# Attention block on one core: the first projection between two query tiles, the residual amid the copies, and the next batch's x tiles and statistics earlier

## The chip, the cores and the metric

The kernel runs on one core of a Trainium2 chip. Times are device microseconds (us) of that core. TensorE (PE) multiplies matrices into PSUM, VectorE (DVE), ScalarE (ACT) and GpSimd (POOL) work on tiles, and SyncE (SP) issues transfers. An engine runs its instructions in the order in which they are written; between engines only semaphores set an order.

## The reference, cut to what matters

```python
def _group_norm(x, scale, bias):                  # 32 groups of 16 channels, over all 1024 tokens
    mean, var = xg.mean(axis=(1, 3)), xg.var(axis=(1, 3))
    return ((xg - mean) * rsqrt(var + EPS)).reshape(B, T, C) * scale + bias

h = _group_norm(x)                                # x: 16 batches of 1024 tokens, 512 channels, fp32
q, k, v = split(h @ qkv_w + qkv_b, 3, axis=-1)    # weight 512 x 1536
q, k, v = (t.reshape(B * 8, 1024, 64) for t in (q * s, k * s, v))
a = softmax(q @ k.T) @ v
out = x + (a.reshape(B, T, C) @ proj_w + proj_b)
```

Because the reshape comes without a transpose, each of the 8 heads of a batch is one block of 128 tokens, whose 512 channels are cut into 8 chunks of 64: 1024 positions of width 64 that attend to one another.

## The kernel before, in words

A batch has 8 blocks (heads), taken as 4 pairs. A block's score matrix has 1024 rows, made 128 at a time: this is a *slot*. A batch has 64 slots, `k` = 0 to 63, the program 1024. All engines run the same loop by *steps* of two slots (even `k`); each has its own list of what it does at which `k`, written out by hand. A pair takes 16 slots, so eight steps; I call them by `k` mod 16: step 0, 2, ..., 14. The stretch "step 4" begins when PE starts the scores of a slot with `k` mod 16 = 4.

In each step PE multiplies the scores of the two slots (L353), which go into two PSUM tiles `s_ps`. Then, in step 2, 6, 10 and 14, it multiplies probabilities by values (`attend`, L382). In step 0, 4, 8 and 12 it transposes two small tiles (L364) and then runs the *large units* of the table `LARGE`: the values `v` of the present pair, the query and key tiles `qk` 0 to 7 of the **next** pair, and the projection of the two blocks of the **previous** pair (`proj` 0 and 1). Twelve units per pair share two PSUM banks, `c_ps0` and `c_ps1`, strictly by turns (`bank`). A unit may start when the unit two places before it has been emptied (`await_bank`).

Who empties a bank depends on the unit. A `qk` tile is emptied by ACT (`stage_qk`): a key tile in one instruction of 128 partitions (L490), a query tile in four of 64 partitions (L495); only the last of them tells PE. `QK_TILES` makes units 0, 1, 4 and 5 query tiles and the rest key tiles. A `proj` unit is emptied by DVE (`take_proj`, L662), which adds it to the residual `x_res`. That tile is loaded by SP (`load_residual`, L306), after the store of the block before has landed, and then given the bias by POOL (`add_bias`, L812); DVE waits for both.

For each slot DVE takes the largest score (L639), ACT the exponential (L475) and DVE turns the result into `turned` in blocks of 32 (L622). After four slots (a *half*) SP moves 16 pieces of `turned` to `probs_t` (L318, `move_half`), which finishes the transpose for `attend`. For the next batch SP loads eight x tiles into one buffer `x_next` (L299), DVE turns each (L611), takes statistics (L707) and aggregates them (L712); PE averages over the groups in `k` = 44 and 46 (L445), reading `s_ps0`, so that the scores after it wait until DVE has taken the product (L717, L724).

Of the kernel before, what the change touches and what calls it, by code (L numbers as in the profile page):

```python
# [11 lines left out]
P = 128  # L12
BATCHES, TOKENS, C = 16, 1024, 512
BLOCKS = TOKENS // P
# [12 lines left out]
Q = 32  # L27
# [4 lines left out]

TURN_STEPS = [4, 8, 12, 20, 24, 28, 36, 40]
STAT_STEPS = [8, 12, 20, 24, 28, 36, 40, 42]
AGGREGATE_SLOT = 42
GROUP_MEAN_SLOT = 44
GROUP_VAR_SLOT = 46

LARGE = {0: [("v", 0), ("v", 1)], 4: [("proj", 0), ("qk", 0), ("qk", 1)],
         8: [("qk", 2), ("qk", 3), ("qk", 4), ("qk", 5)], 12: [("qk", 6), ("proj", 1), ("qk", 7)]}
QK_TILES = [0, 1, 4, 5, 2, 3, 6, 7]
START_TILES = [4, 5, 6, 7, 0, 1, 2, 3]
# [34 lines left out]
def attention_block(nc, x, norm_scale, norm_bias, qkv_w, qkv_b, proj_w, proj_b, out):  # L79
# [3 lines left out]
    with ExitStack() as ctx:  # L83
# [194 lines left out]
        @block.sync  # L278
        def _(sp):
            def load_weight_rows(sp, part, t):  # L280
                cols = slice(part * C, (part + 1) * C)
                for z in range(QUADS):
                    rows = qkv_w[P * z + Q * t:P * z + Q * (t + 1), cols]
                    sp.dma_start(w_stage[t][Q * z:Q * (z + 1), cols], rows).then_inc(w_loaded[part], 16)

            for n in range(2):
                load_x_start(sp, n)
            for part in (1, 0, 2):
                for t in range(KT):
                    load_weight_rows(sp, part, t)  # L290
            for t in range(KT):
                sp.dma_start(pw_stage[t], proj_w[t * P:(t + 1) * P, :]).then_inc(pw_loaded, 16)

            def load_x_tile(b, u):
                if within(b, BATCHES - 1):
                    at_least(sp, xt_turned, BLOCKS * (b + 1) + u)
                    for z in range(QUADS):
                        part = x_t[b + 1, u, :, P * z:P * (z + 1)].rearrange("(a i) c -> i a c", i=Q)
                        sp.dma_start(x_next[Q * z:Q * (z + 1), :].rearrange("p (a c) -> p a c", a=QUADS), part  # L299
                                     ).then_inc(xs_loaded, 16)  # L300

            def load_residual(b, n):
                h = BLOCKS * b + n
                if within(h, N_BLOCKS):
                    at_least(sp, stored, 16 * h)
                    sp.dma_start(x_res[:, :], x_t[b + n // BLOCKS, n % BLOCKS]).then_inc(x_loaded, 16)  # L306

            def move_half(b, k):
                n = (k - MOVE_LAG) // HALF
                half = 2 * BLOCKS * b + n  # L310
                if not within(half, N_HALVES):
                    return
                at_least(sp, probs_turned, HALF * half + HALF)
                at_least(sp, pv_done, half - 1)
                for step in range(QUADS):
                    for a in range(QUADS):
                        to = (a + step) % QUADS
                        sp.dma_start(probs_t[n % 2][Q * to:Q * (to + 1), a, :],  # L318
                                     turned[n % 2][Q * a:Q * (a + 1), to, :]).then_inc(moved[n % 2][to], 16)

            def slot(b, k):
                if k % HALF == MOVE_LAG % HALF:
                    move_half(b, k)
                if k % 16 == 1:
                    load_residual(b, 2 * (k // 16) - 2)
                if k % 16 == 9:
                    load_residual(b, 2 * (k // 16) - 1)
                if k == 1:
                    load_x_tile(b, 0)
                if k - 2 in TURN_STEPS[:-1]:  # L330
                    load_x_tile(b, TURN_STEPS.index(k - 2) + 1)

            batches(slot)
            sp.wait_ge(stored, 16 * N_BLOCKS)

# [135 lines left out]
        def _(act):  # L471
# [61 lines left out]
            def step(b, k):  # L533
                s = SPB * b + k
                if k % HALF == EVAC_LAG % HALF and within(s - EVAC_LAG, N_SLOTS):
                    take_inverse(b, k)
                if within(s, N_SLOTS):
                    softmax_exp(b, k)
                if k % 16 == 8:
                    stage_qk(b, k, 0)  # L540
                if within(s, N_SLOTS):
                    softmax_exp(b, k + 1)
                if k % 16 == 12:
                    stage_qk(b, k, 0)
                if k % 16 == 4:
                    stage_qk(b, k, 1)
                if k % 16 == 4 or k % 16 == 12:
                    stage_qk(b, k, 2)
                if k % 16 == 8:
                    stage_qk(b, k, 1)  # L550
                    stage_qk(b, k, 2)
                    stage_qk(b, k, 3)
                if k % 16 == 6:
                    store(b, 2 * (k // 16) - 2)
                if k % 16 == 14:
                    store(b, 2 * (k // 16) - 1)
                if k % 16 == 0 and within(made_pair(b, k), N_PAIRS):
                    norm_x(b, k, 0)
                    norm_x(b, k, 1)
                if before_start(b) and k == GROUP_VAR_SLOT:  # L560
                    round_qkv_weights(1)
                    round_qkv_weights(0)
                if before_start(b) and k == GROUP_VAR_SLOT + 4:
                    round_qkv_weights(2)
                if b == 0 and k == 0:
                    round_proj_weights()
# [14 lines left out]
        def _(dve):  # L581
# [16 lines left out]
                nc.vector.tensor_scalar(qk_bias[:, KT:2 * KT], qk_bias[:, KT:2 * KT], CH ** -0.5, None,  # L598
                                        ALU.mult).then_inc(bias_scaled, 1)

            def turn_x(b, u):
                if before_start(b):
                    dve.wait_ge(x_start_loaded[u // 2], 16 * QUADS)
                    tile = x_start[u // 2][:, u % 2 * C:(u % 2 + 1) * C]
                else:
                    dve.wait_ge(xs_loaded, 16 * QUADS * (BLOCKS * b + u + 1))
                    tile = x_next[:, :]
                if u % 2 == 0:
                    at_least(dve, h_split, 2 * (PPB * b + u // 2 + 1))
                dst = xt_sb[:, u // 2, :, u % 2 * P:(u % 2 + 1) * P].rearrange("p k (a i) -> p k a i", i=Q)  # L610
                nc.vector.transpose(dst, tile.rearrange("p (a k j) -> p k a j", a=QUADS, k=KT)).then_inc(xt_turned, 1)  # L611

# [51 lines left out]
            def step(b, k):  # L664
# [7 lines left out]
                    turn(b, k)  # L672
                if k % 16 == 0:
                    take_v(b, k, 0)
                if k % 16 == 4:
                    take_proj(b, k, 0)
                if b == 0 and k == 2:
                    split_proj_weights()
                if within(s, N_SLOTS):
                    turn(b, k + 1)  # L680
                if k % 16 == 0:
                    take_v(b, k, 1)
                if k % 16 == 12:
                    take_proj(b, k, 1)
                if k % HALF == HALF - 2 and within(s, N_SLOTS):
                    invert(b, k)
# [5 lines left out]
                if before_start(b) and k == GROUP_VAR_SLOT + 4:  # L692
                    split_qkv_weights(2)

            def statistics(b, k):
                if not within(b + 1, BATCHES):
                    return
                nb = b + 1
                if k in TURN_STEPS:
                    turn_x(b, TURN_STEPS.index(k))  # L700
                if k in STAT_STEPS:
                    u = STAT_STEPS.index(k)
                    dve.wait_ge(xt_turned, BLOCKS * nb + u + 1)
                    if u == 0:
                        at_least(dve, aggregated, 2 * nb)
                    for t in range(KT):
                        last = nc.vector.bn_stats(bn[:, t, u, :], xt_sb[:, u // 2, t, u % 2 * P:(u % 2 + 1) * P])  # L707
                    last.then_inc(bn_done, 1)
                if k == AGGREGATE_SLOT:
                    at_least(dve, bn_done, BLOCKS * (nb + 1))  # L710
                    for t in range(KT):
# [18 lines left out]
        def _(pool):  # L730
# [95 lines left out]
            def four_slots(b, k):  # L826
                m, pair = k % 16, k // 16
                if m == 4:
                    add_bias(b, 2 * pair - 2)
                if m == 12:  # L830
                    add_bias(b, 2 * pair - 1)
                if m == 12:
                    split_qk(b, k, LARGE[m][0][1])
                if m == 8:
                    split_qk(b, k, LARGE[m][0][1])
                    split_qk(b, k, LARGE[m][1][1])
                split_attn(b, (k - EVAC_LAG) // HALF)
                if m == 0 and within(made_pair(b, k), N_PAIRS):
                    split_h(b, k)
                if m == 4:  # L840
                    split_qk(b, k, LARGE[m][1][1])
                if m == 4 or m == 12:
                    split_qk(b, k, LARGE[m][2][1])
                if m == 8:
                    split_qk(b, k, LARGE[m][2][1])
                    split_qk(b, k, LARGE[m][3][1])
                widen_inverse(b, k)
                if k == GROUP_MEAN_SLOT and within(b + 1, BATCHES):
                    affine(b)
# [23 lines left out]
```

## Time and profile before

| | us |
|---|---|
| median of 3 runs (3390.82 to 3396.11) | 3392.52 |
| the profiled execution | 3391.84 |
| its span | 3390.1 |
| busy: PE, DVE, ACT, POOL | 3299.4, 2892.6, 2011.0, 1654.7 |

The span is what lies between the first and the last instruction of the program in the profile; the profiled execution took 1.7 us more. Busy shares are means over the whole span. All 16 batches do the same work, so a stretch of one pair, read instruction by instruction, stands for the others.

### The profile page before, as it was taken

The page shows a single profiled execution, that of the slowest core. Times are in us where ns is not written, and L with a number is a line of the kernel's source. Part 1 is how long each engine was busy: PE and PEld are TensorE (multiplying, and loading weights), DVE is VectorE, ACT ScalarE, POOL GpSimd, SP SyncE. Part 2 cuts the span into 40 slices and gives each one's busy share as a digit, 9 for nine tenths or more (in the row PEclk, how much of TensorE's full clock was granted, in tenths as well). Part 3 has the DMA queues.
Part 4 walks back from the last instruction along what each step waited for, and adds up shares of the span by engine and source line. Part 5 has one row for each costly group of instructions (what it writes and reads, how often), then busy time and mean ns, then how long its engine had stood idle before and what let it go on. Part 6 is the DMA issues. An engine that isn't in the chain of part 4 may idle for free.

```text
span 3390.1 us, 66951 instructions
## 1 busy us (share of the span) xinstructions
PE 3299.4 (97%) x24128; PEld 2488.8 (73%) x24128; DVE 2892.6 (85%) x3601; ACT 2011.0 (59%) x3857; POOL 1654.7 (49%) x2762
## 2 busy tenths in 40 slices
PE   5999999999999999999999999999999999999998
PEld 4777777777777777777777777777777777777775
DVE  5888889888888888888888888888888888888886
ACT  4565565665665656656656666556566565665663
POOL 3454454544545545545545455445454554454552
PEclk9999999999999999999999999999999999999999
DMA  5888878788887888878788787878878888788777
GB/s 115 195 188 197 193 188 203 184 198 192 190 202 184 199 192 193 201 184 201 188 194 202 185 198 188 194 195 190 198 188 197 195 190 201 184 197 194 185 186 183
DMA packets 312633, 646.84 MB, mean 191 GB/s; under 512 B 80624, under 2 KB 146160, under 8 KB 312304
## 3 DMA queue, kind: packets, MB, share of 16 engines
q1 hardware_dynamic: 289216, 607.43, 76.4%
q10 hardware_dynamic: 23088, 35.14, 3.1%
q8 instruction: 192, 3.15, 0.4%
q14 instruction: 137, 1.12, 0.1%
HBM read 71.84 MB, written 33.55 MB: 31 GB/s over the span
## 4 chain that ended last, share of the span: by engine, by line
PE 52%; SPq 32%; DVE 6%; ACT 4%; issue 4%; DMA 1%; POOL 1%; POOLq 0%; DVEq 0%; ACTq 0%
SPq L318 27%; PE pv_ps L382 13%; PE s_ps L353 13%; PE c_ps L418 5%; PE c_ps L419 4%; PE c_ps L420 4%; SPq L299 4%; DVE turned L622 3%; ACT probs L475 2%; PE c_ps L432 2%; PE c_ps L434 2%; PE c_ps L433 2%; ACT staged L495 2%; PE c_ps L400 2%; PE c_ps L401 2%
## 5 line engine op out<-in xcount | busy, mean ns | idle before, releaser
L475 ACT ACTIVATE probs<-s_ps,neg_max 128x1024 f32<-128x1024 f32 x1024 | 1141.3, 1115 | 824.5 <-DVE neg_max L639 821.8
L639 DVE TENSOR_REDUCE neg_max<-s_ps 128x1 f32<-128x1024 f32 x1024 | 1205.1, 1219 | 275.7 <-PE s_ps L353 275.5
L622 DVE STREAM_TRANSPOSE turned<-probs 128x1024 f32<-128x1024 f32 x1024 | 1233.8, 1229 | 92.8 <-ACT probs L475 63.3
L382 PE MATMUL pv_ps<-probs_t,v 128*64 128x256 f32 x8192 | 942.4, 383 | 7.3 <-DMA probs_t<-turned 7.3
L382 PEld LDWEIGHTS pv_ps<-probs_t,v 128*64 128x64 f32 x8192 | 566.4, 137 | 358.6 <-issue 100.1
L418 PE MATMUL c_ps<-h_hi,w_hi 128*128 128x256 f32 x2048 | 595.5, 291 | 35.4 <-DVE x_res L662 15.8
L495 ACT ACTIVATE staged<-c_ps,qk_bias 64x256 f32<-64x256 f32 x1024 | 481.4, 470 | 189.0 <-PE c_ps L420 175.9
L419 PE MATMUL c_ps<-h_lo,w_hi 128*128 128x256 f32 x2048 | 580.6, 283 | 0.0
L420 PE MATMUL c_ps<-h_hi,w_lo 128*128 128x256 f32 x2048 | 579.7, 283 | 0.0
L803 POOL COPY inv_wide<-inv_sum 128x256 f32<-128x256 f32 x256 | 102.1, 399 | 899.4 <-PE pv_ps L364 890.5
L418 PEld LDWEIGHTS c_ps<-h_hi,w_hi 128*128 128x128 f32 x2048 | 393.0, 192 | 47.6 <-DVE x_res L662 20.8
L419 PEld LDWEIGHTS c_ps<-h_lo,w_hi 128*128 128x128 f32 x2048 | 393.7, 192 | 4.3
L420 PEld LDWEIGHTS c_ps<-h_hi,w_lo 128*128 128x128 f32 x2048 | 392.9, 192 | 0.0
L353 PE MATMUL s_ps<-kh,qh_e 64*128 64x512 f32 x1024 | 256.4, 497 | 17.8 <-ACT probs L475 8.8
L490 ACT ACTIVATE staged<-c_ps,qk_bias 128x256 f32<-128x256 f32 x256 | 121.1, 473 | 164.9 <-PE c_ps L420 163.9
L812 POOL TENSOR_TENSOR x_res<-x_res,p_bias 128x512 f32<-128x512 f32 x128 | 165.7, 1295 | 105.9 <-DMA x_res<-in_x 100.8
L353 PEld LDWEIGHTS s_ps<-kh,qh_e 64*128 64x128 f32 x1024 | 96.4, 183 | 160.6 <-issue 91.3
L772 POOL CAST kh<-staged 128x256 fp32r<-128x256 f32 x256 | 102.2, 399 | 218.8 <-ACT staged L490 218.6
L400 PE MATMUL c_ps<-pw_hi,attn_hi 128*128 128x512 f32 x512 | 206.7, 404 | 2.2 <-POOL attn_lo L792 2.2
L432 PE MATMUL c_ps<-w_hi,h_hi 128*128 128x512 f32 x512 | 205.9, 402 | 0.0
L353 PE MATMUL s_ps<-kh,qh_o 64*128 64x512 f32 x1024 | 205.0, 394 | 0.3 <-ACT probs L475 0.3
L353 PE MATMUL s_ps<-kl,qh_e 64*128 64x512 f32 x1024 | 204.9, 395 | 0.0
(68 smaller groups left out, 4984.4 us busy)
## 6 DMA issues: line engine op xcount, KB each, us to landing
probs_t<-turned SPq DMA_DIRECT2D x4096, 128.0 KB, 2.4
x_res<-in_x SPq DMA_DIRECT2D x128, 256.0 KB, 3.0
result<-x_res ACTq DMA_DIRECT2D x128, 256.0 KB, 3.0
x_next<-in_x SPq DMA_DIRECT2D x480, 64.0 KB, 2.4
probs_t<-in_L_conv_qkv_w SPq DMA_DIRECT2D x48, 64.0 KB, 6.0
turned<-in_x SPq DMA_DIRECT2D x8, 128.0 KB, 6.0
turned<-in_x ACTq DMA_DIRECT2D x8, 128.0 KB, 6.3
probs_t<-in_L_conv_proj_w SPq DMA_DIRECT2D x4, 256.0 KB, 3.2
```

The source lines that it names most:

```text
L318: sp.dma_start(probs_t[n % 2][Q * to:Q * (to + 1), a, :], turned[n % 2][Q * a:Q * (a + 1), to, :]).then_inc(moved[n % 2][to], 16)
L353: last = nc.tensor.matmul(s_ps[k % 2][:, par * C:(par + 1) * C], q[c % 2][rows, at, c // 2, :], keys[rows, at, :, :].rearrange("p j t -> p ...
L382: last = nc.tensor.matmul(pv_ps[side][CH * par:CH * (par + 1), 0, :], v_sb[:, ring_of(i, parity), CH * chunk:CH * (chunk + 1)], p_t[:, par ...
L400: nc.tensor.matmul(c[:, :], a_hi, pw_hi[:, j, :], start=(j == 0), stop=False)
L418: nc.tensor.matmul(c[:, 0:2 * P], wh, h_hi[:, t, :], start=(t == 0), stop=False)
L419: nc.tensor.matmul(c[:, 0:2 * P], wh, h_lo[:, t, :], start=False, stop=False)
L420: last = nc.tensor.matmul(c[:, 0:2 * P], wl, h_hi[:, t, :], start=False, stop=(t == KT - 1))
L432: nc.tensor.matmul(c[:, :], hh, w_hi[:, t, 2 * C:3 * C], start=(t == 0), stop=False)
L475: nc.scalar.activation(probs[k % 2][:, :], s_ps[k % 2][:, :], ACT.Exp, bias=neg_max[:, k % 4:k % 4 + 1], accum_out=row_sum[:, (k // HALF) ...
L495: last = nc.scalar.activation(staged[n % 2][to, par, :], c[of, 0:2 * P], ACT.Identity, bias=qk_bias[of, tile:tile + 1])
L622: nc.vector.transpose(dst, probs[k % 2][:, :].rearrange("p (k b j) -> p k b j", k=CHUNKS, b=QUADS)).then_inc(probs_turned, 1)
L639: nc.vector.tensor_reduce(neg_max[:, k % 4:k % 4 + 1], s_ps[k % 2][:, :], AX.X, ALU.max, negate=True).then_inc(max_ready, 1)
```

## The change

Four things are edited. (1) In step 4 the projection comes second in place of first: `qk` 0, `proj` 0, `qk` 1. So `qk` 0 and `qk` 1 now share `c_ps0`, and `proj` 0 has `c_ps1`. DVE adds that projection behind both turnings of the step, not between them; ACT and POOL take `qk` 0 at the places that step 12 already had. (2) SP loads the residual after the first 8 of a half's 16 copies, not after all. (3) The x tiles and statistics of a batch are spread anew over the steps: tiles 0 and 1 already in the batch before. (4) The statistics are aggregated at `k` = 40, not 42.

```diff
-TURN_STEPS = [4, 8, 12, 20, 24, 28, 36, 40]
-STAT_STEPS = [8, 12, 20, 24, 28, 36, 40, 42]
-AGGREGATE_SLOT = 42
+LOAD_AT = {42: (0, 2), 54: (1, 2), 58: (2, 2), 6: (3, 1), 10: (4, 1), 22: (5, 1), 26: (6, 1), 38: (7, 1)}
+TURN_AT = {52: (0, 2), 56: (1, 2), 4: (2, 1), 8: (3, 1), 20: (4, 1), 24: (5, 1), 36: (6, 1), 40: (7, 1)}
+STAT_AT = {56: (0, 2), 60: (1, 2), 8: (2, 1), 12: (3, 1), 24: (4, 1), 28: (5, 1), 36: (6, 1), 40: (7, 1)}
+AGGREGATE_SLOT = 40
-LARGE = {0: [("v", 0), ("v", 1)], 4: [("proj", 0), ("qk", 0), ("qk", 1)],
+LARGE = {0: [("v", 0), ("v", 1)], 4: [("qk", 0), ("proj", 0), ("qk", 1)],
...
# SP, slot(b, k)
                 if k % HALF == MOVE_LAG % HALF:
-                    move_half(b, k)
-                if k % 16 == 1:
-                    load_residual(b, 2 * (k // 16) - 2)
-                if k % 16 == 9:
-                    load_residual(b, 2 * (k // 16) - 1)
-                if k == 1:
-                    load_x_tile(b, 0)
-                if k - 2 in TURN_STEPS[:-1]:
-                    load_x_tile(b, TURN_STEPS.index(k - 2) + 1)
+                    move_half(b, k, (0, 1))
+                    if k % 16 == 0:
+                        load_residual(b, 2 * (k // 16) - 2)
+                    if k % 16 == 8:
+                        load_residual(b, 2 * (k // 16) - 1)
+                    move_half(b, k, (2, 3))
+                if k in LOAD_AT:
+                    load_x_tile(b + LOAD_AT[k][1], LOAD_AT[k][0])
...
# ACT, step(b, k)
-                if k % 16 == 12:
+                if k % 16 == 4 or k % 16 == 12:
                     stage_qk(b, k, 0)
-                if k % 16 == 4:
-                    stage_qk(b, k, 1)
...
# DVE, step(b, k)
-                if k % 16 == 4:
-                    take_proj(b, k, 0)
                 if b == 0 and k == 2:
                     split_proj_weights()
                 if within(s, N_SLOTS):
                     turn(b, k + 1)
                 if k % 16 == 0:
                     take_v(b, k, 1)
-                if k % 16 == 12:
+                if k % 16 == 4 or k % 16 == 12:
                     take_proj(b, k, 1)
...
# DVE, statistics(b, k)
+                if before_start(b) and k == 0:
+                    for u in range(2):
+                        turn_x(0, u)
+                    for u in range(2):
+                        take_statistics(0, u)
+                if k in TURN_AT:
+                    turn_x(b + TURN_AT[k][1], TURN_AT[k][0])
+                if k in STAT_AT:
+                    take_statistics(b + STAT_AT[k][1], STAT_AT[k][0])
...
# POOL, four_slots(b, k)
-                if m == 12:
+                if m == 4 or m == 12:
                     split_qk(b, k, LARGE[m][0][1])
...
-                if m == 4:
-                    split_qk(b, k, LARGE[m][1][1])
```

How the instructions stand on the engines is shown at three places. The first is ACT in a step 4: the two exponentials, then the eight instructions that empty the two query tiles. Before:

```order
L475 ACTIVATE probs1,row_sum<-s_ps1,neg_max 128x1024 [waits max_ready]
L495 ACTIVATE staged0<-c_ps1,qk_bias 64x256 [waits qk_ready,qk_full]
L495 ACTIVATE staged0<-c_ps1,qk_bias 64x256 x3
L495 ACTIVATE staged1<-c_ps0,qk_bias 64x256 [waits qk_ready,qk_full]
L495 ACTIVATE staged1<-c_ps0,qk_bias 64x256 x3
```

and now:

```order
L476 ACTIVATE probs1,row_sum<-s_ps1,neg_max 128x1024 [waits max_ready]
L496 ACTIVATE staged0<-c_ps0,qk_bias 64x256 [waits qk_ready,qk_full]
L496 ACTIVATE staged0<-c_ps0,qk_bias 64x256 x3
L496 ACTIVATE staged1<-c_ps0,qk_bias 64x256 [waits qk_ready,qk_full]
L496 ACTIVATE staged1<-c_ps0,qk_bias 64x256 x3
```

The order on ACT has not moved; both tiles now come out of the same bank, `c_ps0`, so PE can't fill it for the second until four instructions have emptied it of the first.

The second place is PE in the same step, where the last unit begins. Before, `qk` 0 in `c_ps1` ends and `qk` 1 begins:

```order
L418 MATMUL c_ps1<-h_hi,w_hi 128x256
L419 MATMUL c_ps1<-h_lo,w_hi 128x256
L420 MATMUL c_ps1<-h_hi,w_lo 128x256
L418 MATMUL c_ps0<-h_hi,w_hi 128x256 [waits out_ready]
L419 MATMUL c_ps0<-h_lo,w_hi 128x256
```

and now, where `proj` 0 in `c_ps1` ends and `qk` 1 begins:

```order
L401 MATMUL c_ps1<-pw_hi,attn_hi 128x512
L402 MATMUL c_ps1<-pw_lo,attn_hi 128x512
L403 MATMUL c_ps1<-pw_hi,attn_lo 128x512
L419 MATMUL c_ps0<-h_hi,w_hi 128x256 [waits qk_staged]
L420 MATMUL c_ps0<-h_lo,w_hi 128x256
```

The unit is the same, but it waits for ACT (`qk_staged`) where it waited for DVE's sum (`out_ready`).

The third place is DVE at `k` = 42 and the first half of `k` = 44. Before:

```order
L622 STREAM_TRANSPOSE turned0<-probs1 128x8x4x32 [waits probs_ready]
L629 RECIPROCAL inv_sum<-row_sum 128x4 [waits inv_widened]
L707 BN_STATS bn<-xt_sb 128x6 [waits xt_turned]
L707 BN_STATS bn<-xt_sb 128x6 x3
L712 BN_AGGR mv<-bn 128x2 [waits bn_done]
L712 BN_AGGR mv<-bn 128x2 x3
L639 TENSOR_REDUCE neg_max<-s_ps0 128x1 [waits scores_full]
```

and now:

```order
L623 STREAM_TRANSPOSE turned0<-probs0 128x8x4x32 [waits probs_ready]
L623 STREAM_TRANSPOSE turned0<-probs1 128x8x4x32 [waits probs_ready]
L630 RECIPROCAL inv_sum<-row_sum 128x4 [waits inv_widened]
L640 TENSOR_REDUCE neg_max<-s_ps0 128x1 [waits scores_full]
L640 TENSOR_REDUCE neg_max<-s_ps1 128x1 [waits scores_full]
```

The eight small instructions ahead of the reduction are gone from there; the last four statistics and the aggregation now stand at the end of `k` = 40, behind the turning of tile 7.

## Rows read from the trace of the kernel before

**Rows 1.** The page: the span, and busy time of each engine with its share.

```profile
span 3390.1 us, 66951 instructions
PE 3299.4 (97%) x24128; PEld 2488.8 (73%) x24128; DVE 2892.6 (85%) x3601; ACT 2011.0 (59%) x3857; POOL 1654.7 (49%) x2762
```

**Rows 2.** Waits on PE, the largest after the start: us in total, times, longest.

```profile
PE c_ps L418 <- DVE x_res L662: 15.8, 23, 1.5
```

**Rows 3.** Timeline of PE, two steps 4: start, length, what, [idle before].

```profile
1518.58 0.50 PE L353 MATMUL s_ps<-kh,qh_e 64*128 64x512 f32 x2
...
1526.18 0.50 PE L353 MATMUL s_ps<-kh,qh_e 64*128 64x512 f32 x2
...
1569.62 0.50 PE L353 MATMUL s_ps<-kh,qh_e 64*128 64x512 f32 x2
...
1576.76 0.39 PE L418 MATMUL c_ps<-h_hi,w_hi 128*128 128x256 f32 x1 [0.91 <-DVE x_res L662]
...
1578.39 0.50 PE L353 MATMUL s_ps<-kh,qh_e 64*128 64x512 f32 x2
```

**Rows 4.** Timeline of POOL and DVE in the second of these steps.

```profile
1574.62 1.29 POOL L812 TENSOR_TENSOR x_res<-x_res,p_bias 128x512 f32<-128x512 f32 x1 [2.42 <-DMA x_res<-in_x]
1576.01 0.69 DVE L662 TENSOR_TENSOR x_res<-c_ps,x_res 128x512 f32<-128x512 f32 x1 [1.44 <-POOL x_res L812]
```

**Rows 5.** Timeline of SP's transfer issues ahead of that step.

```profile
1558.12 2.02 SPq L299 DMA_DIRECT2D x_next<-in_x  x4
1560.23 11.14 SPq L318 DMA_DIRECT2D probs_t<-turned  x16
1571.42 0.58 SPq L306 DMA_DIRECT2D x_res<-in_x  x1
```

**Rows 6.** Timeline of PE, a step 12 of the same batch.

```profile
1544.25 0.50 PE L353 MATMUL s_ps<-kh,qh_e 64*128 64x512 f32 x2
...
1550.28 0.28 PE L418 MATMUL c_ps<-h_hi,w_hi 128*128 128x256 f32 x1
...
1551.80 0.50 PE L353 MATMUL s_ps<-kh,qh_e 64*128 64x512 f32 x2
```

**Rows 7.** Timeline of ACT: the first step 4 and that step 12.

```profile
1520.86 1.12 ACT L475 ACTIVATE probs<-s_ps,neg_max 128x1024 f32<-128x1024 f32 x1 [1.79 <-DVE neg_max L639]
...
1546.51 1.12 ACT L475 ACTIVATE probs<-s_ps,neg_max 128x1024 f32<-128x1024 f32 x1 [1.77 <-DVE neg_max L639]
...
1548.75 0.47 ACT L490 ACTIVATE staged<-c_ps,qk_bias 128x256 f32<-128x256 f32 x1
```

**Rows 8.** Timeline of PE, DVE and ACT in the step of `k` = 44.

```profile
1647.59 0.50 PE L353 MATMUL s_ps<-kh,qh_e 64*128 64x512 f32 x2
...
1653.62 0.28 PE L445 MATMUL s_ps<-mv,group_avg 128*128 128x8 f32 x2
...
1654.35 0.39 PE L418 MATMUL c_ps<-h_hi,w_hi 128*128 128x256 f32 x1 [0.44 <-ACT staged L490]
...
1656.09 0.49 PE L353 MATMUL s_ps<-kh,qh_e 64*128 64x512 f32 x2
...
1649.42 1.06 DVE L712 BATCH_NORM_AGGREGATE mv<-bn 128x2 f32<-128x48 f32 x4
1650.40 2.29 DVE L639 TENSOR_REDUCE neg_max<-s_ps 128x1 f32<-128x1024 f32 x2
...
1653.83 0.47 ACT L490 ACTIVATE staged<-c_ps,qk_bias 128x256 f32<-128x256 f32 x1
```

**Rows 9.** Timeline of DVE, the reductions of `k` = 42 in that batch.

```profile
1643.40 2.36 DVE L639 TENSOR_REDUCE neg_max<-s_ps 128x1 f32<-128x1024 f32 x2 [1.01 <-PE s_ps L353]
```

**Rows 10.** Timeline of the start: DVE before the first scores, then ACT and PE.

```profile
15.06 0.83 DVE L707 BATCH_NORM_STATS2 bn<-xt_sb 128x6 f32<-128x128 f32 x4
...
72.47 1.91 ACT L495 ACTIVATE staged<-c_ps,qk_bias 64x256 f32<-64x256 f32 x4
...
71.58 0.50 PE L353 MATMUL s_ps<-kh,qh_e 64*128 64x512 f32 x2 [0.97 <-ACT probs L475]
```

More of the change, by code:

```diff
@@ L292, in _, with load_x_tile @@
                 sp.dma_start(pw_stage[t], proj_w[t * P:(t + 1) * P, :]).then_inc(pw_loaded, 16)
-            def load_x_tile(b, u):
-                if within(b, BATCHES - 1):
-                    at_least(sp, xt_turned, BLOCKS * (b + 1) + u)
+            def load_x_tile(nb, u):
+                if 0 < nb < BATCHES:
+                    at_least(sp, xt_turned, BLOCKS * nb + u)
                     for z in range(QUADS):
-                        part = x_t[b + 1, u, :, P * z:P * (z + 1)].rearrange("(a i) c -> i a c", i=Q)
+                        part = x_t[nb, u, :, P * z:P * (z + 1)].rearrange("(a i) c -> i a c", i=Q)
                         sp.dma_start(x_next[Q * z:Q * (z + 1), :].rearrange("p (a c) -> p a c", a=QUADS), part
@@ L306, in load_residual, with move_half @@
                     sp.dma_start(x_res[:, :], x_t[b + n // BLOCKS, n % BLOCKS]).then_inc(x_loaded, 16)
-            def move_half(b, k):
+            def move_half(b, k, steps):
                 n = (k - MOVE_LAG) // HALF
@@ L314, in move_half @@
                 at_least(sp, pv_done, half - 1)
-                for step in range(QUADS):
+                for step in steps:
                     for a in range(QUADS):
@@ L599, in scale_bias, with turn_x @@
                                         ALU.mult).then_inc(bias_scaled, 1)
-            def turn_x(b, u):
-                if before_start(b):
+            def turn_x(nb, u):
+                if not within(nb, BATCHES):
+                    return
+                if nb == 0:
                     dve.wait_ge(x_start_loaded[u // 2], 16 * QUADS)
@@ L605, in turn_x @@
                 else:
-                    dve.wait_ge(xs_loaded, 16 * QUADS * (BLOCKS * b + u + 1))
+                    dve.wait_ge(xs_loaded, 16 * QUADS * (BLOCKS * (nb - 1) + u + 1))
                     tile = x_next[:, :]
                 if u % 2 == 0:
-                    at_least(dve, h_split, 2 * (PPB * b + u // 2 + 1))
+                    at_least(dve, h_split, 2 * (PPB * (nb - 1) + u // 2 + 1))
                 dst = xt_sb[:, u // 2, :, u % 2 * P:(u % 2 + 1) * P].rearrange("p k (a i) -> p k a i", i=Q)
@@ L693, in step, with take_statistics @@
                     split_qkv_weights(2)
-            def statistics(b, k):
+            def take_statistics(nb, u):
+                if not within(nb, BATCHES):
+                    return
+                dve.wait_ge(xt_turned, BLOCKS * nb + u + 1)
+                if u == 0:
+                    at_least(dve, aggregated, 2 * nb)
+                for t in range(KT):
+                    last = nc.vector.bn_stats(bn[:, t, u, :], xt_sb[:, u // 2, t, u % 2 * P:(u % 2 + 1) * P])
+                last.then_inc(bn_done, 1)
+            def statistics(b, k):
+                if before_start(b) and k == 0:
[7 more added lines that the diff above has]
+                    take_statistics(b + STAT_AT[k][1], STAT_AT[k][0])
                 if not within(b + 1, BATCHES):
@@ L698, in statistics @@
                 nb = b + 1
[L699 to L708, printed above, removed]
                 if k == AGGREGATE_SLOT:
```

## The prediction

> **What bounds the kernel now.** I read the page first: PE is busy 3299.4 of 3390.1 us, 97%, DVE 85% [rows 1]. So a change here can win only what PE stands idle, and can lose wherever it makes PE stand. The second view is the list of waits on PE: outside the first and last few steps they are few. The largest is the `qk` multiplication that waits for DVE's sum of the projection, 23 times, 15.8 us in all [rows 2].
>
> The third view is PE's timeline, step by step. A step 4 without a wait lasts 1526.18 - 1518.58 = 7.60 us. One with the wait lasts 1578.39 - 1569.62 = 8.77, though the idle time put down is 0.91 [rows 3]. So one wait costs its idle time and 0.26 more, since the last product was still counted as busy beyond the next one's usual start, and the restart is slower. All 23 cost 15.8 + 23 x 0.26 = 21.8 us. Who is late is in the rows of the same step: POOL waited 2.42 us for the residual, added the bias until 1575.91, DVE added the projection until 1576.70, and PE went on at 1576.76 [rows 4]. The residual was issued at 1571.42, behind 16 copies that took 11.14 us, and these behind an x tile's 2.02 [rows 5]. SP is what is late.
>
> The rest of PE's time is products one behind another, so each step keeps its length unless its waits change. I take each edit by what it does to the length of one step.
>
> **The change part by part.**
>
> *Residual amid the copies, sum later.* Eight copies take 11.14 / 2 = 5.57 us [rows 5]; by so much sooner the residual is issued. In the step shown that is 1565.85, and as it took until about 1574.6 from 1571.42, it lands at 1569.1, while POOL was ready for it at 1574.62 - 2.42 = 1572.20 [rows 4]. POOL's bias is then done at 1573.5, 3.9 into the step, and DVE's sum, now behind both turnings, comes after the projection itself, some 6 us into the step as in step 12. It frees `c_ps1`, which PE needs next in step 8, two steps later. So these waits go: **-21.8 us**. Behind the sum on DVE only an x tile and the next reductions queue, which wait for the next scores anyway. What the residual costs SP is nothing new, one issue of 0.58 [rows 5], except at the very end, where the last copies come 0.6 later: **+0.6**.
>
> *Projection between the two query tiles.* PE's work stays, its wait doesn't. `qk` 1 now needs `c_ps0` empty of `qk` 0, and that is ACT's work behind both exponentials. Step 12 already has this order (`qk`, `proj`, `qk`), and shows both sides. On PE the last unit starts 1550.28 - 1544.25 = 6.03 into the step and the step lasts 7.55 [rows 6]. On ACT the staging begins at 1548.75, 4.50 into the step, straight behind the exponentials [rows 7]. There it is a key tile: one instruction, 0.47, done at 4.97, a full 1.06 early. In step 4 it is a query tile: four instructions, 1.91 us [rows 10]. The exponentials start 2.28 into step 4, against 2.26 into step 12 [rows 7], since they hang on this step's scores; so staging begins at 4.52 and ends at 6.43. PE goes on 0.05 after such an end (ACT done at 1653.83 + 0.47 = 1654.30, PE at 1654.35 [rows 8]), at 6.48, where it could at 6.03. From the restart to the next scores it is 1578.39 - 1576.76 = 1.63 [rows 3]. The new step 4 lasts 6.48 + 1.63 = 8.11 in place of 7.60: +0.51. It happens in each pair that has both a next pair to make and a projection: 64 less the first and the last, 62. **+31.6 us**. Nothing downstream gives it back: the next reductions, exponentials and turnings start from the next scores, which are late with it.
>
> In the first pair, where there is no projection between the two tiles, `qk` 1 stands directly behind `qk` 0. ACT came to the staging at 72.47 [rows 10], so PE would go on at 72.47 + 1.91 + 0.05 and reach the next scores 1.63 later, at 76.06, where it did at 71.58. That is 4.5 at most; PE waited for ACT there too (0.97), so some of it was lost before as well. I take **+2.5** of 0 to 4.5.
>
> *Statistics forward.* At `k` = 44 the step lasts 1656.09 - 1647.59 = 8.50, of which the group product is one part and a wait for ACT's staging of `qk` 6 the other [rows 8]. The cause is DVE: its reduction starts at 1650.40, behind the aggregation, 2.81 into the step [rows 8], where 1.0 is usual (in step 42 it is at 1643.40, after 1.01 idle [rows 9]). Exponentials and staging follow, 1.8 late. With the aggregation gone from there the staging ends near 1652.5, before the projection does, and the step is that of step 12, 7.55, and the product. Its two matmuls start at 1653.62 and fill 0.28 [rows 8]; I take 0.25, between 0 (hidden) and the whole 0.73 until PE went on. So 7.80, a gain of 0.70 in 15 batches: **-10.5 us**, between 3.3 and 14.3. The wait for the second product, at `k` = 46, starts from that step's scores and stays.
>
> The aggregation (1.06 [rows 8]) now stands ahead of the reduction of `k` = 42, which had 1.01 to spare [rows 9]. It is 0.05 late, and I allow 0.2 more for the semaphore waits between. I cost it at nothing, since ACT is still staging the last query tiles of step 8 when that reduction ends; without this cover it is 0.25 x 15 = 3.8.
>
> *Loads and turnings of x.* The same count on SP and DVE, spread evenly: two loads in each pair in place of up to four. SP's pair is then 64 copies at 11.14 / 16 = 0.70, two residuals and two loads: 44.6 + 1.2 + 4.0 = 49.8 us, of the 3390.1 / 64 = 53.0 that a pair takes on average [rows 1], so it keeps up. At the start one block of statistics, 0.83 [rows 10], falls into a time in which DVE waited for x anyway: **-0.8**.
>
> The sum: -21.8 + 0.6 + 31.6 + 2.5 - 10.5 - 0.8 = **+1.6 us**. On the profiled execution's 3391.84 that is 3393.4; the median of the runs, 3392.52, is 0.7 above this execution, so **3394**. What a measurement of this kernel can tell from no change is 0.2%, 6.8 us: the forecast is no change that can be told, by two large terms that cancel.
>
> **A rule against a row.** A restart behind a wait took 1.63 where the same twelve products took 1551.80 - 1550.28 = 1.52 without [rows 3, 6], so the first weights were not in place when the wait ended. The Trainium skill's page "TensorE: Matmul & The Clock Gate", section "What happens when you issue a matmul", says that PE pulls the loading of weights ahead of products still in flight. By that rule qk 1's weights would wait in the array and the restart would cost nothing; by the row it costs 0.11 each time. I go by the row.
>
> **The rivals.**
>
> *Restart hidden.* If the restart is as short as 1.52, the sum is less by 62 x 0.11 = 6.8: 3387. The two rows speak against it. It would still be no change. Chance 0.08.
>
> *Faster: the bank is free in time.* If ACT had staged `qk` 0 by 6.03, step 4 would last 7.55: 62 x -0.05 = -3.1 in place of +31.6, and no first-pair loss: 3357. It takes staging 0.40 earlier, so exponentials at 1.9 into the step; they start from this step's own scores in both steps shown, 0.02 apart. Half way there it would be about 3376. Chance 0.08 for both.
>
> *Slower: SP held among its copies.* The residual waits for the store of the block before. It stands now in the middle of a half's copies, so if the store lands late, eight copies stand behind it, then DVE's turning into that buffer, then everything. The store is issued in step 6 or 14, before the turnings of that step, and SP comes to the residual 5.57 us after the last of them; so the store has those 5.57 us and more to land. It decides where it takes longer; at 0.3 us per pair beyond what the copies have to spare it is 62 x 0.3 = 19: 3413. Chance 0.08.
>
> *Slower: the wait at `k` = 44 stays* in another form, DVE being late from `k` = 40 on, and the 10.5 are not won: 3405. It decides where the reduction of 44 starts over 1 us late. Chance 0.08.
>
> *The residual still comes late.* Then the first edit wouldn't do what it says, but PE would not see it, since it needs that bank two steps later. The time is the forecast's.
>
> **How the numbers follow.** The forecast has 0.68, the last case within it. Its own terms move by 62 x 0.05 = 3 (offsets read to 0.02 or 0.03, two of them), 4 for the product, 2 for the first pair: 3389 to 3400. For 8 in 10 the range takes in the hidden restart and the stay of 44's wait: **3386 to 3405**. Faster by over 0.2% (below 3385.7): 0.12, the free bank and a part of the lower edge. Slower (above 3399.3): 0.21. The same: 0.67.
>
> **What would show it.** In the changed profile PE's waits for DVE's sum are gone, and those of the `qk` line for ACT's query staging (L496) stand some 60 times, about 0.3 us idle each, some 18 us in all. A step 4 lasts 8.1 in every pair, `k` = 44 7.8, step 12 still 7.55. POOL's wait for the residual (2.42 in the step shown) is gone. If the steps 4 last 7.55, the order on ACT has not the price that I give it, and the kernel is faster. If PE waits for copies, or DVE's turnings do, SP was held. If `k` = 44 still lasts 8.5, the statistics were not what delayed it.

## The result, and the profile after

The changed kernel takes **3394.89 us** (median of 20 runs, 3392.99 to 3396.61), the kernel before 3389.85 (20 runs beside them, 3381.02 to 3396.11): ratio **1.0018, 95% interval 1.0011 to 1.0025**. That is 0.18%, inside the 0.2% that counts as no change here, though its upper end passes it. (The two medians alone give 1.0015.) The forecast was 3394.

The page of the changed kernel: the span, the busy times, and the chain of work that ended last, by engine; then that chain for the kernel before.

```profile
span 3393.7 us, 67205 instructions
PE 3308.8 (97%) x24128; PEld 2481.5 (73%) x24128; DVE 2898.6 (85%) x3601; ACT 2005.8 (59%) x3857; POOL 1656.2 (49%) x2762
...
PE 84%; ACT 7%; DVE 5%; issue 2%; SPq 1%; DMA 0%; POOL 0%; ACTq 0%; POOLq 0%
...
PE 52%; SPq 32%; DVE 6%; ACT 4%; issue 4%; DMA 1%; POOL 1%; POOLq 0%; DVEq 0%; ACTq 0%
```

The profiled execution is 3.6 us longer than that of before [rows 1]. SP's queue has 1% of the chain that ended last, where it had 32%. Most of its place went to PE (52% to 84%); ACT, which has the query staging (L496), went from 4% to 7%.

Waits on PE after: us in total, times, longest.

```profile
PE c_ps L419 <- ACT staged L496: 24.2, 65, 5.3
...
PE s_ps L354 <- DVE gvar L732: 8.4, 15, 0.6
```

The wait for DVE's sum [rows 2] is gone from the list. In its place stand 65 waits for the query staging: two at the start (3.2 us together), one of 5.3 in the first pair, and 62 of 0.25 in the steps 4. One of those on PE's timeline, the step that [rows 3] show first for before:

```profile
1520.34 0.50 PE L354 MATMUL s_ps<-kh,qh_e 64*128 64x512 f32 x2
...
1526.17 0.39 PE L403 MATMUL c_ps<-pw_hi,attn_lo 128*128 128x512 f32 x1
1526.81 0.39 PE L419 MATMUL c_ps<-h_hi,w_hi 128*128 128x256 f32 x1 [0.25 <-ACT staged L496]
...
1528.44 0.50 PE L354 MATMUL s_ps<-kh,qh_e 64*128 64x512 f32 x2
```

And ACT, POOL and DVE in the same step:

```profile
1522.61 1.12 ACT L476 ACTIVATE probs<-s_ps,neg_max 128x1024 f32<-128x1024 f32 x1 [1.78 <-DVE neg_max L640]
...
1524.85 1.91 ACT L496 ACTIVATE staged<-c_ps,qk_bias 64x256 f32<-64x256 f32 x4
...
1522.87 1.29 POOL L820 TENSOR_TENSOR x_res<-x_res,p_bias 128x512 f32<-128x512 f32 x1
...
1526.60 0.69 DVE L663 TENSOR_TENSOR x_res<-c_ps,x_res 128x512 f32<-128x512 f32 x1 [0.28 <-PE c_ps L403]
```

Read from the step's start at 1520.34: exponentials at 2.27, staging from 4.51 to 6.42, PE on at 6.47, next scores 1.63 later, at 8.10. DVE's sum is at 6.26, behind both turnings, and POOL's bias no longer waits, where it did for 2.42 [rows 4].

The step of `k` = 44, on PE, DVE and ACT (before: [rows 8]):

```profile
1649.60 0.50 PE L354 MATMUL s_ps<-kh,qh_e 64*128 64x512 f32 x2
...
1655.63 0.28 PE L446 MATMUL s_ps<-mv,group_avg 128*128 128x8 f32 x2
1655.77 0.36 PE L419 MATMUL c_ps<-h_hi,w_hi 128*128 128x256 f32 x1
...
1657.37 0.50 PE L354 MATMUL s_ps<-kh,qh_e 64*128 64x512 f32 x2
...
1650.60 2.35 DVE L640 TENSOR_REDUCE neg_max<-s_ps 128x1 f32<-128x1024 f32 x2
...
1654.10 0.47 ACT L491 ACTIVATE staged<-c_ps,qk_bias 128x256 f32<-128x256 f32 x1
```

It lasts 1657.37 - 1649.60 = 7.77, and PE passes from the group product to the next `qk` unit without a wait: the reduction starts 1.00 into the step, where it was 2.81, and staging ends at 4.97.

Where the 3.6 us are, by the lengths of the same steps in both traces:

| stretch | before | after | difference |
|---|---|---|---|
| start, to the first scores | 52.95 | 53.15 | +0.2 |
| first five steps of the first pair (`k` = 0 to 8) | 33.97 | 37.71 | +3.7 |
| steps 4 of the other 62 pairs | 493.2 | 502.2 | +9.0 |
| `k` = 44, 15 batches | 8.50 each | 7.77 each | -10.9 |
| step `k` = 58 of the last batch | 5.63 | 7.17 | +1.5 |
| behind the last scores | 34.2 | 34.4 | +0.2 |

The 493.2 of before are 62 x 7.60 = 471.2 and 22.0 of waiting; the 502.2 of after are 62 x 8.10.

### The profile page after: what moved, and what is told of

Same layout as the page of the kernel before. It is cut to its first block, busy times and chain, and to the rows that moved or that the text cites. A ratio compares the mean times of both kernels' runs of the same rounds, so it can differ in the third digit from the quotient of the medians.

```text
span 3393.7 us, 67205 instructions
## 1 busy us (share of the span) xinstructions
PE 3308.8 (97%) x24128; PEld 2481.5 (73%) x24128; DVE 2898.6 (85%) x3601; ACT 2005.8 (59%) x3857; POOL 1656.2 (49%) x2762
## 4 chain that ended last, share of the span: by engine, by line
PE 84%; ACT 7%; DVE 5%; issue 2%; SPq 1%; DMA 0%; POOL 0%; ACTq 0%; POOLq 0%
PE pv_ps L383 25%; PE s_ps L354 22%; PE c_ps L419 7%; PE c_ps L420 6%; PE c_ps L421 6%; ACT staged L496 4%; PE c_ps L433 3%; PE c_ps L435 3%; PE c_ps L434 3%; ACT probs L476 3%; DVE neg_max L640 3%; PE pv_ps L365 2%; PE c_ps L401 2%; PE c_ps L402 2%; PE c_ps L403 2%
## 5 line engine op out<-in xcount | busy, mean ns | idle before, releaser
L419 PE MATMUL c_ps<-h_hi,w_hi 128*128 128x256 f32 x2048 | 604.5, 295 | 34.3 <-ACT staged L496 24.2
L496 ACT ACTIVATE staged<-c_ps,qk_bias 64x256 f32<-64x256 f32 x1024 | 480.6, 469 | 188.5 <-PE c_ps L421 176.8
L419 PEld LDWEIGHTS c_ps<-h_hi,w_hi 128*128 128x128 f32 x2048 | 393.7, 192 | 64.4 <-ACT staged L496 50.9
L778 POOL CAST qh_e<-staged 128x256 fp32r<-128x256 f32 x256 | 102.0, 399 | 225.8 <-ACT staged L496 225.8
```

Of the source, the lines that this page charges most:

```text
L419: nc.tensor.matmul(c[:, 0:2 * P], wh, h_hi[:, t, :], start=(t == 0), stop=False)
L496: last = nc.scalar.activation(staged[n % 2][to, par, :], c[of, 0:2 * P], ACT.Identity, bias=qk_bias[of, tile:tile + 1])
```

## The experiments

All six compute the whole of the reference. Each ratio is to the kernel before, run beside it on the same chip. To tell what each edit does: X is the new times of x loads, turnings and statistics, R the residual amid the copies, O the new order in step 4 with the sum behind both turnings.

**A key tile first in step 4 (all of X, R and O).** The order of units stays `qk`, `proj`, `qk`, but the first `qk` makes a key tile, which ACT stages in one instruction.

```
-QK_TILES = [0, 1, 4, 5, 2, 3, 6, 7]
+QK_TILES = [4, 0, 5, 6, 1, 2, 7, 3]
...
+                if k % 16 == 4 and tile >= KT and not before_start(b):
+                    pool.wait_ge(scores_full, SPB * b + k + 4)
```

POOL also splits that tile later in its step, behind `split_attn`, since the scores still read the old key halves. Expected:

> The changed kernel, with the first unit of step 4 a key tile in place of a query tile (the order of the eight tiles becomes key, query, key, key, query, query, key, query); POOL splits that key tile behind the attention split and waits until the scores of the pair's first eight slots are done, since they still read the old keys. Theory (the price is ACT's four staging instructions ahead of the second query tile in the same bank): staging ends about 5.0 us into the step, a step 4 lasts 7.55 and not 8.10, so 62 x 0.55 = 34 us less and about 1.5 in the first pair: 3359. Rival (the price is the place of the projection or the restart of PE, whatever ACT stages): 3395, steps 4 stay at 8.1.

Measured: 3362.07 us (3361.11 to 3362.98), ratio 0.9917, interval 0.9902 to 0.9932. Steps 4 last 7.55 to 7.58 in all 62 pairs. ACT in step 4 of the same batch as above, then the waits on PE that name a staging:

```profile
1510.22 0.47 ACT L491 ACTIVATE staged<-c_ps,qk_bias 128x256 f32<-128x256 f32 x1
...
PE c_ps L419 <- ACT staged L491: 5.8, 3, 3.6
...
PE c_ps L419 <- ACT staged L496: 3.2, 2, 2.6
```

The staging begins 4.51 into the step (its scores start at 1505.71), as in the changed kernel, but is done 0.47 later and not 1.91, and the 62 waits are gone; of the five left, four lie within the first 74 us. With the projection still in the middle this is worth 33 us, so it is not the order of the units that costs, but four staging instructions between two users of one bank.

**The other way round: a query tile first in step 12 too.** The changed kernel with two tiles exchanged:

```
-QK_TILES = [0, 1, 4, 5, 2, 3, 6, 7]
+QK_TILES = [0, 1, 4, 5, 2, 6, 3, 7]
```

> The changed kernel with the tiles of the last two units exchanged in the list QK_TILES: the first qk unit of step 12 (number 6) makes a query tile, of four staging instructions, and the third (number 7) a key tile, of one. Step 4 is untouched. Theory: what a step loses is set by what ACT has to stage between the two qk units that share a bank, so step 12 becomes like step 4: 7.55 to 8.10, 63 x 0.55 = 35 us more than the changed kernel's 3395, some 3430 us, with some 126 waits of the qk line for the query staging. Rival: step 4 loses because of what goes before it there (its exponentials, POOL, or the first pair tile being split), not because of the staging; then step 12 keeps its 7.55 and the time stays near 3395.

Measured: 3426.29 us (3423.38 to 3428.98), ratio 1.0103, interval 1.0088 to 1.0118. Steps 12 go from 7.55 to 8.07, and the step of `k` = 44, which is one of them, from 7.77 to 8.07. Waits on PE, then ACT and PE in a step 12 that starts at 1562.13:

```profile
PE c_ps L419 <- ACT staged L496: 39.1, 113, 5.1
...
1566.63 1.90 ACT L496 ACTIVATE staged<-c_ps,qk_bias 64x256 f32<-64x256 f32 x4
...
1568.58 0.39 PE L419 MATMUL c_ps<-h_hi,w_hi 128*128 128x256 f32 x1 [0.26 <-ACT staged L496]
```

Staging from 4.50 to 6.40, PE on at 6.45: the same numbers as in step 4. The 15 steps `k` = 44 pay only 0.30: the group product fills most of the wait there (0.14 us of idle time is left in the step of batch 7), and the list has 48 more waits than the changed kernel's 65. The price follows the query tile.

**O alone.** The kernel before with the new order of step 4 and nothing else:

```
-LARGE = {0: [("v", 0), ("v", 1)], 4: [("proj", 0), ("qk", 0), ("qk", 1)],
+LARGE = {0: [("v", 0), ("v", 1)], 4: [("qk", 0), ("proj", 0), ("qk", 1)],
```

> The kernel before with the new order of step 4 alone. Theory: no wait of PE on DVE's sum, though the residual comes as late as before, since the bank is wanted two steps later; steps 4 at 8.1 everywhere, the step of k = 44 still at 8.5: 3394.9 + 11 = 3406. Rival (the late residual delays DVE, and so the scores behind it): above 3415, steps of other lengths than 8.1 at k = 20 and 36.

Measured: 3404.37 us (3402.98 to 3404.90), ratio 1.0041, interval 1.0026 to 1.0056. Steps 4 last 8.10 everywhere and `k` = 44 8.50. The waits for DVE's sum are gone although residual and x loads stand where they stood: the later place of the sum covers a late residual by itself, and costs 502.1 - 471.2 = 30.9 to save 22.0. At the start, its first scores come 0.7 later (53.63), with the first product where it was (32.23).

**X and R without O.** The changed kernel with before's order of step 4:

```
-LARGE = {0: [("v", 0), ("v", 1)], 4: [("qk", 0), ("proj", 0), ("qk", 1)],
+LARGE = {0: [("v", 0), ("v", 1)], 4: [("proj", 0), ("qk", 0), ("qk", 1)],
```

> The changed kernel with the order of step 4 as before (projection first, its sum between the two turnings), all else changed. Theory: steps 4 at 7.60 with no wait, the residual being early: 3394.9 - 62 x 0.50 - 3.6 in the first pair - 0.9 at the start = 3359. Rival (the order's price is small and the gain of the early residual is what was lost): 3390 or above.

Measured: 3358.44 us (3357.06 to 3359.41), ratio 0.9905, interval 0.9888 to 0.9921. Steps 4 last 7.60 without a wait, `k` = 44 7.77. Against the changed kernel's own profiled execution it is 36.1 us shorter (3357.6 to 3393.7), which is what O costs where nothing is late: 502.2 - 470.9 = 31.3 in the 62 steps 4, 3.7 in the first pair, 0.7 at the start.

**R alone.** The kernel before with the residual amid the copies:

```
                 if k % HALF == MOVE_LAG % HALF:
-                    move_half(b, k)
-                if k % 16 == 1:
-                    load_residual(b, 2 * (k // 16) - 2)
+                    move_half(b, k, (0, 1))
+                    if k % 16 == 0:
+                        load_residual(b, 2 * (k // 16) - 2)
...
+                    move_half(b, k, (2, 3))
```

> The kernel before with the residual amid the copies alone. Theory: the residual comes 5.6 us earlier, more than it was ever late (at most 1.7), so PE's waits on DVE's sum go, steps 4 last 7.60, and the kernel gains what these waits cost in a mean run, about 20 us: 3370, with a narrower spread of its runs. Rival (x tiles pile up on SP in k = 1 to 16 and it stays late, or the copies behind the residual hold DVE): 3380 to 3392.

Measured: 3380.24 us (3374.23 to 3386.15, 10 runs), ratio 0.9971, interval 0.9962 to 0.9980. My theory, 3370, fell. Steps 4 are still late in 14 of 62 pairs, 8.4 us in all, and single runs still differ by 12 us. The residual is not what is late there. Waits on POOL and DVE; then, around a step 4 (`k` = 36 of batch 8) that starts at 1818.82, SP's issues, DVE and PE:

```profile
POOL x_res L813 <- DMA x_res<-in_x: 7.4, 1, 7.4
...
DVE turned L623 <- DMA probs_t<-turned: 24.4, 33, 2.1
...
1793.65 3.64 SPq L299 DMA_DIRECT2D x_next<-in_x  x4
1797.39 10.35 SPq L318 DMA_DIRECT2D probs_t<-turned  x16
1807.78 2.01 SPq L299 DMA_DIRECT2D x_next<-in_x  x4
1809.89 6.08 SPq L318 DMA_DIRECT2D probs_t<-turned  x8
1816.01 0.59 SPq L306 DMA_DIRECT2D x_res<-in_x  x1
1816.70 5.58 SPq L318 DMA_DIRECT2D probs_t<-turned  x9
...
1824.16 1.25 DVE L623 STREAM_TRANSPOSE turned<-probs 128x1024 f32<-128x1024 f32 x1 [1.63 <-DMA probs_t<-turned]
1825.33 0.65 DVE L663 TENSOR_TENSOR x_res<-c_ps,x_res 128x512 f32<-128x512 f32 x1
...
1826.03 0.39 PE L419 MATMUL c_ps<-h_hi,w_hi 128*128 128x256 f32 x1 [0.99 <-DVE x_res L663]
```

POOL waits for a residual only once, in the last pair. But the second eight copies now stand behind the residual (the first eight of the nine from 1816.70), DVE's turning waits for them before it may write `turned` again, and the sum stands behind that turning. SP was late as before; the edit only moved its lateness from the residual to the copies. It is late in a pattern: in the kernel before, all 26 late steps 4 are `k` = 20 (15 of them) and `k` = 36 (11), the ones behind the pairs into which SP also loads four and three x tiles; here they are 7 and 7 at the same places. SP's own lag shows the same: in the kernel before, the first of the copies that follow a pair's last four slots goes out 2.84 us behind the turning that it waits for in a batch's first pair, 2.06 in the second and 0.03 in the third and fourth (means of 15 batches).

**X alone.** So the loads themselves are the suspect. The kernel before with the new times of loads, turnings and statistics, the residual behind all sixteen copies, and the old order:

```
+LOAD_AT = {42: (0, 2), 54: (1, 2), 58: (2, 2), 6: (3, 1), 10: (4, 1), 22: (5, 1), 26: (6, 1), 38: (7, 1)}
...
-AGGREGATE_SLOT = 42
+AGGREGATE_SLOT = 40
```

> The kernel before with the new times of the x loads, turnings and statistics alone; the residual still goes out behind all sixteen copies, and step 4 keeps its old order. All theories: k = 44 lasts 7.8 in place of 8.5, 15 x 0.7 = 10.5 us gained. If what makes the residual late is the row of up to four x tiles that SP loads within one pair, spreading them over all pairs takes its waits away as well: steps 4 at 7.60 everywhere, about 3358 us, the same as with the residual amid the copies (3358.4), and the place of the residual is then worth nothing. If the copies ahead of it are what makes it late, a part of the waits stays: 3365 to 3378, and single runs again spread over some 10 us.

Measured: **3356.88 us** (3356.64 to 3358.59), ratio 0.9900, interval 0.9884 to 0.9917. The waits on PE between the start and the last pair (60 to 3270 us):

```profile
PE s_ps L353 <- DVE gvar L735: 8.4, 15, 0.6
PE s_ps L353 <- ACT probs L475: 7.0, 4, 3.9
PE c_ps L418 <- ACT staged L490: 1.6, 1, 1.6
```

Every step 4 behind the first pair lasts 7.60, `k` = 44 7.77. X alone does all that the three edits win, and the spread of single runs shrinks from 9 us to 2. X also moves DVE's turnings and statistics, and no run moves the loads without them; but what is late in the kernel before is SP, and its lag is now 0.13, 0.04, 0.04 and 0.03 us in the four pairs. The residual still comes late at times, as POOL waits for it 22 times, 30.7 us (before: 56 times, 100.8), but no longer so late that PE feels it. By the profiled executions, steps 4 give 22.3, `k` = 44 gives 10.9, and the first scores come 2.9 earlier, which is the clock's in part (last section). This is the best version; against X and R together (3358.44, on another chip) the difference is too small to say that R does harm, but no gain of it shows.

## Why the prediction came out

**Right, with its sizes.** *Projection between the two query tiles*: the step was worked out from a step 12 and four staging instructions as 8.11 and lasts 8.10; the two `QK_TILES` runs show that the cause is the count of staging instructions between two users of `c_ps0`. 62 steps cost 502.2 - 471.2 = 31.0, forecast 31.6. *The waits for the residual*: 21.8 forecast, 22.0 measured in the execution that the forecast read. *Statistics forward*: 10.5 forecast, 15 x 0.73 = 10.9 measured, and the aggregation ahead of `k` = 42 costs nothing. The forecast sum was +1.6 and the profiled execution grew by 3.6; of the 2.0 between, 1.5 is the step `k` = 58 of the last batch, for which no term stood.

**In range, but not as worked out.** *First pair*: 3.7 over five steps, in the allowed 0 to 4.5. But the step of `k` = 4 alone grew by 5.7, from 7.22 to 12.92, and 2.1 came back in the step behind it. On PE in that step:

```profile
74.76 0.58 PE L419 MATMUL c_ps<-h_hi,w_hi 128*128 128x256 f32 x1 [5.28 <-ACT staged L496]
...
77.62 0.79 PE L354 MATMUL s_ps<-kh,qh_e 64*128 64x512 f32 x2
```

The wait ended 0.33 later than forecast (74.43), as ACT's staging began 0.33 later, but from there to the next scores it took 2.86 and not 1.63. The granted clock reads 0.50 from 74 to 78 us, the lower level, behind PE's stand of 5.28. I had taken the restart from a step at the upper level. Over the five steps the granted clock is 0.80, and was 0.88 before. With O alone, which has the same step of 12.92, it is 0.90, and the five steps grow by 1.8 only (33.97 to 35.78).

**Wrong, a term's sign.** *The start*, -0.8: DVE's aggregation does come earlier, and PE's first product behind it too (31.51, before 32.23), but the new order holds for the first `qk` tiles as well, where no projection stands between the two tiles of one bank. PE then waits 0.56 for ACT, and the first scores come 0.2 later than before. I had charged that wait only to the first pair; O alone shows the same, with first scores 0.7 later. (Some of the 0.2 may be the clock's, last section.) *The end*, +0.6, was +0.2 behind the last scores.

**Wrong, a cause.** *Residual amid the copies, sum later* got all 21.8, and *Loads and turnings of x* got 0. For the kernel as changed the sum is the same, since the waits go either way; for the parts it is not. The step that failed is that I counted SP's pair only for the new schedule, 49.8 of 53.0 us. With the old one, by the same count, a pair with four x loads is an estimated 44.6 + 1.2 + 4 x 2.02 = 53.9 and one with three 51.9, and a pair of eight steps without waits lasts 51.0 (8.50 - 7.55 more where it has `k` = 44): SP falls behind in just these two (2.84 and 2.06 us at their ends). The rows for it were in [rows 5]. X alone wins the 22.0, R alone 13.6 of them, and O alone, by the sum's later place, also all of them, at a price of 30.9. Three edits removed one loss, and the dearest one was needed by none.

**The rivals.** *Bank free in time* is refuted for this tile order by 62 steps of 8.10, and becomes true with a key tile first. *Restart hidden*: the restart is 1.63 us in the step shown, against the 1.52 of [rows 6]. The rows of the weight loads say why, first the load of the product at 1526.81, then all of that line:

```profile
1526.81 0.19 PEld L419 LDWEIGHTS c_ps<-h_hi,w_hi 128*128 128x128 f32 x1 [0.68 <-ACT staged L496]
...
L419 PEld LDWEIGHTS c_ps<-h_hi,w_hi 128*128 128x128 f32 x2048 | 393.7, 192 | 64.4 <-ACT staged L496 50.9 <-issue 7.8 <-ACT staged L491 2.6
```

The load begins together with its product, and 50.9 us of idle time before such loads are put down to the staging. The Trainium skill's page "TensorE: Matmul & The Clock Gate", section "What happens when you issue a matmul", lets a load run ahead of products in flight; here it did not run ahead of the wait, which stands ahead of it in the program (`await_bank`). So that rule was no reason to expect a restart at no cost. *SP held among its copies*: step `k` = 58 of the last batch grew by 1.5, but it lasts 7.2 also with X alone and with O alone, where the residual stands behind the copies, so this is not that mechanism; why the one execution of before had 5.63 there is open. PE's waits for copies are 7.7 us in all, 7.3 before. *The wait at `k` = 44 stays*: it doesn't. *The residual still comes late*: POOL waits for it once (8.0 us), where it did 56 times (100.8).

**The median.** The forecast went by an execution of 3391.84 and three runs around 3392.5; over 20 runs before's median is 3389.85. So the medians differ by 5.0, and the two profiled executions by 3.6. That 3394 lies within 0.9 of the median is luck: the base was 2.7 too high and the change 3.4 too small. Before's runs lie 15 us apart and those of the changed kernel 3.6. The likely reason is that SP is not equally late in each run: the two kernels in which PE waits for SP, before and R alone, spread by 15 and 12 us, the six others by 2 to 6. One trace of each kernel can't show it.

## What to carry to other kernels

When a unit is put between two users of one buffer, don't ask whether there is more time between them, but whether what empties the buffer is done by then, with its real count of instructions: one staging instruction was done 1.06 us before PE could use the bank, four were done 0.39 after. Work out a queue's load for the old schedule too, pair by pair; where a transfer is late, look first for what else the queue was given in that stretch (here the x tiles), before moving the late transfer within it. And when several edits aim at one loss, run each alone: here X wins 36 us (3392.91 to 3356.88 on one chip), and O gives them back (3357.6 to 3393.7, the profiled executions of X and R and of all three).

## What was not expected of the hardware

At the start, products of 256 columns first stand 0.21 us apart and then 0.12, as at the lower and the upper of TensorE's two levels, 1.2 and 2.4 GHz. The granted clock reads 1.00 on both sides of this first change (31 to 48 us), so the spacing alone shows it. Its moment differs between the eight profiled executions, one of each kernel. PE's timeline of the changed kernel, then of X alone, around that moment:

```profile
40.54 0.41 PE L420 MATMUL c_ps<-h_lo,w_hi 128*128 128x256 f32 x1
40.75 0.40 PE L421 MATMUL c_ps<-h_hi,w_lo 128*128 128x256 f32 x1
40.97 0.30 PE L419 MATMUL c_ps<-h_hi,w_hi 128*128 128x256 f32 x1
41.11 0.28 PE L420 MATMUL c_ps<-h_lo,w_hi 128*128 128x256 f32 x1
41.23 0.28 PE L421 MATMUL c_ps<-h_hi,w_lo 128*128 128x256 f32 x1
```

```profile
36.77 0.41 PE L418 MATMUL c_ps<-h_hi,w_hi 128*128 128x256 f32 x1
36.98 0.35 PE L419 MATMUL c_ps<-h_lo,w_hi 128*128 128x256 f32 x1
37.17 0.27 PE L420 MATMUL c_ps<-h_hi,w_lo 128*128 128x256 f32 x1
37.28 0.28 PE L418 MATMUL c_ps<-h_hi,w_hi 128*128 128x256 f32 x1
37.40 0.28 PE L419 MATMUL c_ps<-h_lo,w_hi 128*128 128x256 f32 x1
```

Both had begun that run of products at 34.1 and 34.0. In the eight profiled kernels the change comes 3.1 to 7.7 us behind that beginning. Later, PE waits 2.6 us for ACT ahead of the last twelve products before the first scores. In X alone these stand 0.12 apart all the same (granted clock 1.00 from 44 to 51 us); in the changed kernel they are 0.21 apart from the fifth on (granted clock 0.77 from 48 to 54). X alone reaches its first scores at 50.05, X and R at 52.41. So 2 or 3 us of these executions are set at the start, by no edit that I can name; whether executions of one kernel differ by as much, one trace of each can't show.
